# Graph network, three layers of segment maximum: two whole columns of each step fetched row by row by SyncE and ScalarE, their offsets loaded 16 and 32 at a time

## The reference: what is computed

```python
def _sage_conv(x, src, dst, Wl, bl, Wr):
    agg = jax.ops.segment_max(x[src], dst, num_segments=x.shape[0])
    agg = jnp.where(jnp.isfinite(agg), agg, 0.0)
    return agg @ Wl + bl + x @ Wr
...
h = jnp.maximum(_layernorm(x, axis=-1), 0.0)
x = x + _L0_gnn_ref(h, edge_index, ...)     # three _sage_conv, each with a leaky ReLU behind it
```

## Time and profile before

| | |
|---|---|
| median of three runs | 6050.79 us |
| the profiled execution | 6050.56 us, of which the span from first to last instruction is 6048.9 us |
| GpSimd busy | 4524.8 us (75%) |
| VectorE busy | 2893.5 us (48%) |
| ScalarE busy | 225.4 us (4%) |
| TensorE busy (matmul) | 732.5 us (12%) |

### The profile page before, as it was taken

How to read it: one execution, slowest core, us unless ns; L and a number is a source line. 1 busy time by engine, 2 the same in 40 slices (tenths; PEclk the granted TensorE clock), 3 DMA queues, 4 the chain that set the end, 5 groups by cost and what they waited for, 6 DMA issues and landing times.

```text
span 6048.9 us, 53349 instructions
## 1 busy us (share of the span) xinstructions
PE 732.5 (12%) x2214; PEld 411.8 (7%) x2214; DVE 2893.5 (48%) x3638; ACT 225.4 (4%) x664; POOL 4524.8 (75%) x4793
## 2 busy tenths in 40 slices
PE   1111111111100311111111110040010000100003
PEld 0000000000000200000000000030000000000002
DVE  5333333333333555555555555565555555555556
ACT  1000000000000100000000000010000000000001
POOL 6777777777777777777777777767777777777776
PEclk7555555555555655555555555575555555555556
DMA  4333333333333566666666666666666666666665
GB/s 141 108 111 107 108 108 109 110 108 108 108 108 107 171 216 218 218 216 220 216 218 218 216 219 214 215 206 219 217 220 215 218 218 216 220 215 218 215 216 175
DMA packets 461123, 1089.10 MB, mean 180 GB/s; under 512 B 116295, under 2 KB 181740, under 8 KB 461068
## 3 DMA queue, kind: packets, MB, share of 16 engines
q0 software_dynamic: 203520, 519.10, 30.6%
q1 hardware_dynamic: 220508, 544.04, 24.8%
q10 hardware_dynamic: 37040, 25.45, 1.5%
HBM read 555.08 MB, written 533.07 MB: 180 GB/s over the span
## 4 chain that ended last, share of the span: by engine, by line
POOL 49%; issue 17%; DMA 1%; POOLq 1%; DVE 0%; PE 0%; DVEq 0%
POOL ring L448 47%; POOL ring L475 2%; POOLq L444 0%; DMA ring<-running_max_log,end_row 0%; POOLq L441 0%; DMA patch<-running_max_log,patch_row 0%; DMA ring<-features,stage 0%; DMA running_max_log<-patch 0%; POOL patch L465 0%; DVE z_sum L902 0%; DVE agg L894 0%; POOLq L455 0%; POOLq L443 0%; DMA features<-h_out 0%; DVE patch L873 0%
## 5 line engine op out<-in xcount | busy, mean ns | idle before, releaser
L448 POOL DMA_INDIRECT ring<-features,stage x4611 | 4360.0, 946 | 1432.2 <-issue 1383.7
L792 DVE TENSOR_TENSOR ring<-banks,ring 128x1024 f32<-128x1024 f32 (+1 forms) x1173 | 1227.4, 1046 | 2954.0 <-DMA ring<-features,stage 2918.9
L758 DVE TENSOR_TENSOR banks<-ring,banks 128x1024 f32<-128x1024 f32 (+1 forms) x1173 | 1232.1, 1050 | 37.5
L975 PE MATMUL banks<-wr,h_turned 128*128 128x256 f32 (+1 forms) x490 | 220.7, 596 | 3623.4 <-ACT h_turned L1109 3623.4
L975 PEld LDWEIGHTS banks<-wr,h_turned 128*128 128x128 f32 x490 | 127.2, 320 | 3687.4 <-ACT h_turned L1109 3678.6
L991 PE MATMUL banks<-dst_low,own 128*128 128x394 bf16 x200 | 100.4, 502 | 976.0 <-DVE own L734 976.0
L475 POOL DMA_INDIRECT ring<-running_max_log,end_row x147 | 142.9, 972 | 65.6 <-issue 43.9
L1109 ACT ACTIVATE h_turned<-banks 128x256 f32<-128x256 f32 (+1 forms) x147 | 51.8, 353 | 3128.6 <-issue 2664.1
L739 DVE COPY stage<-edges 128x8 int32 (+1 forms) x588 | 119.4, 203 | 88.0 <-DVE banks L758 32.8
L977 PE MATMUL banks<-b,ones 1*128 1x256 f32 (+1 forms) x294 | 157.6, 637 | 0.0
L1048 PE MATMUL banks<-wl,agg 128*128 128x256 f32 (+1 forms) x490 | 110.7, 369 | 1.2 <-DVE agg L894 0.9
(11 more groups left out here) (114 smaller groups left out, 523.4 us busy)
## 6 DMA issues: line engine op xcount, KB each, us to landing
running_max_log<-ring SPq DMA_DIRECT2D x782, 512.0 KB, 3.1
running_max_log<-ring SPq DMA_DIRECT2D x391, 256.0 KB, 2.2
ring<-features ACTq DMA_DIRECT2D x4752, 1.0 KB
ring<-features,stage POOLq DMA_INDIRECT x4611, 3.2
ring<-features SPq DMA_DIRECT2D x3888, 1.0 KB
ring<-features ACTq DMA_DIRECT2D x2376, 0.5 KB
ring<-features SPq DMA_DIRECT2D x1944, 0.5 KB
h_in<-features ACTq DMA_DIRECT2D x98, 128.0 KB, 2.5
```

The costliest lines, as they stand in the source:

```text
L448: pool.indirect_dma_start(ring[0:rows, c * w:(c + 1) * w], None, tables[l], bass.IndirectOffsetOnAxis(ap=stage[0:rows, b, u:u + 1].bitcast ...
L758: dve.tensor_tensor(sum_ps[:, 0:CHAINS * w].rearrange("p (h f) -> p h f", h=CHAINS), group(g - 1).rearrange("p (h f) -> p h f", h=CHAINS), ...
L792: dve.tensor_tensor(group(g), sum_ps[:, 0:CHAINS * w], group(g), ALU.max).then_inc(turn, 1)
L975: pe.matmul(mm_ps[p][:, 0:n], h_turned[p][:, c, :], wr_sb[l][:, c, :], start=(c == 0), stop=False)
```

## The change

Columns 54 and 55 of each full step are fetched row by row as a whole: SyncE fetches the 128 rows of column 55, ScalarE the 128 rows of column 54. GpSimd gathers 54 columns of a full step and no longer the part of column 54. SyncE loads 16 offsets at a time (eight loads in a step, behind the first eight logs), ScalarE 32 at a time (four loads). The offsets of a batch begin at multiples of 16 or 32 of their tensor, and a row of that tensor is 256 words in place of 160. The last step of a layer is as before.

```diff
-SYNC_ROWS, SYNC_AT_ONCE = 72, 8
-ACT_AT_ONCE = 11
-ROWS = 160
+FETCHED_COLS = 2
+SYNC_ROWS = 128
+AT_ONCE, ACT_AT_ONCE = 16, 32
...
+    ROWS = FETCHED_COLS * P
     ROWS_OF = [(0, SYNC_ROWS), (SYNC_ROWS, ROWS - SYNC_ROWS)]
...
-        return width(b, last) - (b == BLOCKS - 1 and not last)
+        return width(b, last) - (FETCHED_COLS if b == BLOCKS - 1 and not last else 0)
...
-            rows = 2 * P - ROWS if c == RING_COLS - 2 and not last else P
             pool.indirect_dma_start(
-                ring[0:rows, c * w:(c + 1) * w], None, tables[l],
+                ring[:, c * w:(c + 1) * w], None, tables[l],
...
-                    first = g * SYNC_AT_ONCE
+                    first = g * AT_ONCE
...
-                            if not last and BLOCK_GROUPS * b * SYNC_AT_ONCE < SYNC_ROWS:
+                            if not last and BLOCK_GROUPS * b * AT_ONCE < SYNC_ROWS:
                                 fetch_rows(i, BLOCK_GROUPS * b)
```

More of the change, by code:

```diff
@@ L87, in gnn_program @@
     assert LAST <= RING_COLS - CHAINS and all(f * (STEPS - 1) < 1 << 16 for f in FETCHED)
-    assert SYNC_ROWS % SYNC_AT_ONCE == 0 and (ROWS - SYNC_ROWS) % ACT_AT_ONCE == 0
-    assert SYNC_ROWS // SYNC_AT_ONCE <= GROUPS - 3
+    assert SYNC_ROWS % AT_ONCE == 0 and (ROWS - SYNC_ROWS) % ACT_AT_ONCE == 0
+    assert SYNC_ROWS // AT_ONCE <= GROUPS - 3
     def by_pool(b, last):
-        return width(b, last) - (b == BLOCKS - 1 and not last)
+        return width(b, last) - (FETCHED_COLS if b == BLOCKS - 1 and not last else 0)
     OPENING = [CHAINS if b == LATE_BLOCK else width(b, True) for b in range(BLOCKS)]
@@ L278, in gnn_program @@
         LAYERS = len(shapes)
-        LOADS = 8
+        LOADS = 6 + FETCHED_COLS
         CONSTS = 16 + 2 * CHAINS
@@ L307, in run_neighbours, with lists_of @@
             return pairs
[L309 to L316, removed]
+        def lists_of(edges_src):
+            return [(row_list[:, k * P:(k + 1) * P],
+                     bass.AP(edges_src.tensor, (CHAINS - 1 - k) * P * RUN + GROUPS - 1, [[GROUPS, STEPS - 1], [RUN, P]]))
+                    for k in range(FETCHED_COLS)]
         def row_places(k, engine, i, at, count, w):
@@ L331, in row_slot @@
         def row_slot(k, r, w):
-            before, p = divmod(ROWS_OF[k][0] + r, P)
-            c = RING_COLS - 1 - before
-            p += before * (2 * P - ROWS)
+            ahead, p = divmod(ROWS_OF[k][0] + r, P)
+            c = RING_COLS - 1 - ahead
             return ring[p:p + 1, c * w:(c + 1) * w].bitcast(U8)
@@ L414, in _ @@
                         pool.dma_start(dest, there).then_inc(sort_done, DMA)
-                pool.wait_ge(list_loaded, 2 * DMA)
+                pool.wait_ge(list_loaded, FETCHED_COLS * DMA)
                 with nc.allow_non_contiguous_dma(reason="one word of each row to fetch"):
-                    for here, there in list_of(sorted_src):
+                    for here, there in lists_of(sorted_src):
                         pool.dma_start(here, there).then_inc(sort_done, DMA)
@@ L446, in gather @@
                             c = b * BLOCK_COLS + u
-                            rows = 2 * P - ROWS if c == RING_COLS - 2 and not last else P
                             pool.indirect_dma_start(
-                                ring[0:rows, c * w:(c + 1) * w], None, tables[l],
+                                ring[:, c * w:(c + 1) * w], None, tables[l],
                                 bass.IndirectOffsetOnAxis(
-                                    ap=stage[0:rows, b, u:u + 1].bitcast(U32), axis=0),
+                                    ap=stage[:, b, u:u + 1].bitcast(U32), axis=0),
                             ).then_inc(late_landed if last and b == LATE_BLOCK and u >= CHAINS else landed[b], DMA)
@@ L689, in _ @@
             dve.memset(restart_turns[:, :, 0], LOWEST).then_inc(prep_done, 1)
-            dve.wait_ge(list_loaded, 2 * DMA)
+            dve.wait_ge(list_loaded, FETCHED_COLS * DMA)
             for w in widths:
@@ L1207, in _ @@
             with nc.allow_non_contiguous_dma(reason="one word of each row to fetch"):
-                for here, there in list_of(src):
+                for here, there in lists_of(src):
                     sp.dma_start(here, there).then_inc(list_loaded, DMA)
@@ L1228, in fetch_rows @@
                             sp.wait_ge(logged[BLOCKS - 1], i * (DMA * STORES_OF[BLOCKS - 1]) + LOGGED[BLOCKS - 1] * l)
-                    places = row_places(0, mybir.EngineType.SP, i, first, SYNC_AT_ONCE, w)
+                    places = row_places(0, mybir.EngineType.SP, i, first, AT_ONCE, w)
                     for r, place in enumerate(places):
@@ L1247, in log_step @@
                                      ).then_inc(logged[b], DMA)
-                        if not last and (BLOCK_GROUPS * b + 1) * SYNC_AT_ONCE < SYNC_ROWS:
+                        if not last and (BLOCK_GROUPS * b + 1) * AT_ONCE < SYNC_ROWS:
                             fetch_rows(i, BLOCK_GROUPS * b + 1)
```

## The result

The changed kernel takes 6475.25 us (median of four runs, 6472.84 to 6482.3) against 6051.17 us for the kernel before (four runs): a ratio of 1.0703, interval 1.0685 to 1.0722. The forecast was 6350 us, in a range of 5945 to 6600. The profiled execution took 6473.37 us. From its page: the span; the groups that answer to the earlier trace rows, with busy time, mean ns, idle time and its releaser; the instruction queue (packets, MB, share); and the logs' KB and us to landing, which answer to the earlier trace rows.

What follows compares the result with a forecast made beforehand. The prediction took GpSimd's gathers to bound the kernel, and the row fetch with its piled logs to bound it afterwards. From 6050.6 us, +332 for layers 2 and 3 and −34 for layer 1 gave 6350 us, range 5945 to 6600.

Steps and rivals of the forecast that it cites:

- the chain: Layers 2 and 3, from row fetch through group 13's log to the next fetch: 76.1 us a round (70.7 to 81.9).
- the burst of six logs: Sign of being right: on SyncE, six logs go out behind its last row, near 65 us of a step.
- SyncE's rows: SyncE's fetch of 128 rows with eight loads of 16 offsets: 63.6 us a step (58.2 to 69.4).
- The piled logs: Logs of groups 8 to 13 queue behind SyncE's rows: 12.5 us from last row to next fetch, layers 2 and 3.
- ScalarE's rows: ScalarE's fetch of 128 rows with four loads of 32: 56 to 72 us, likely 61 to 63.
- GpSimd as the bound before: In the kernel before, GpSimd's 55 gathers of 1.25 us set the step at 68.75 us; the row fetch is hidden.
- The floor of 54 gathers: With one gather fewer, GpSimd alone needs 67.5 us for a full step.
- The sum: Whole kernel against the profiled 6050.6 us: −34 in layer 1, +166 in each of layers 2 and 3, giving 6349.
- the 26 rounds: Layers 2 and 3: 26 rounds lengthened from 68.75 to 76.1 us, 191 us in each layer.
- GpSimd stays the bound: Rival: SyncE's chain in layers 2 and 3 stays under 67.5 us, all 101 us are saved, 5949 us; chance 0.20.
- The two cancel: Rival: loads of 16 take 1.4 us, logs as counted; 6057 us, within 0.2% of no change; chance 0.07.
- A price for each register: Rival: wide loads cost 0.27 us per register, so ScalarE takes 84 us a step; about 7900 us; chance 0.06.

Runs made afterwards that it cites:

- e2: e1 with SyncE's eight batches of rows behind the logs of groups 0, 1, 3, 5, 6, 8, 10 and 11, so nearly none pile up: 6479.32 us.
- e4: The kernel before the change, with only ScalarE's offset loads widened to 32, 32 and 24, aligned, instead of eight of 11: 6054.21 us, ratio 0.9999.
- e1: The changed kernel with 33 do-nothing semaphore increments on SyncE ahead of its first layer, shifting its loops: 6361.42 us, ratio 1.0508.
- e6: e1 with each of SyncE's eight loads of 16 offsets ahead of its log instead of behind it: 6145.06 us, ratio 1.0142.
- e5: The changed kernel with its offsets stored one word further on, so no load begins at a multiple of four words: 7937.73 us in one run.
- e10: e8 with do-nothing semaphore increments on SyncE and ScalarE that shift both engines' loops: 6060.8 us, ratio 1.0011.
- e3: e1 with SyncE loading 32 offsets four times instead of 16 eight times, rows still issued 16 behind each log: 6170.01 us, ratio 1.0189.
- e7: e6 with ScalarE's first load of a step also ahead of its waits: 6086.75 us, ratio 1.0053.
- e11: e10 with SyncE's eight batches behind the logs of groups 0, 1, 2, 4, 5, 7, 8 and 10: 6115.2 us, ratio 1.0103.
- e12: e7 (128 rows on each engine) with SyncE's batches behind the logs of groups 0, 1, 2, 4, 5, 7, 8 and 10: 6177.47 us, ratio 1.0205.
- e9: e8 with 112 rows on SyncE and 144 on ScalarE: 6385.22 us, ratio 1.0549.
- e8: e7 with SyncE fetching 120 of the 256 rows and ScalarE 136: 6163.45 us, ratio 1.0182.

## Why the prediction was right, and what it mis-sized

The mechanism came as forecast. In layer 3, which no refetch disturbs, the chain goes round in 76.0 us against 76.1, and the burst of six logs stands behind SyncE's last row.

- **SyncE's rows.** 47.0 us and eight loads of 2.1 us: 63.6 with the first load. Measured from the first load's start to the last row's end 64.1; the loads 2.15 us at the median, 1.6 in layer 1 (1.8 was taken).
- **The piled logs.** 12.5 us were forecast from the last row to the next fetch; layer 3 has 11.9, which by the forecast's own terms is 1.7 for each of the six logs where 1.8 was taken. The log of group 13 lands 6.8 us behind its issue. e2 shows the mechanism by itself: without the pile that landing is 3.1 us, and the tail 4.1 us shorter.
- **ScalarE's rows.** 61 to 63 us were forecast, 53 to 56 came: the load of 32 was mis-sized, 2.25 us and not 3.3, and the 128 rows without loads take 46 us where their upper bound of 50 was put in. It costs the total nothing, since SyncE ends later.
- **GpSimd as the bound before.** e4 takes 18 us from ScalarE's queue for a ratio of 0.9999. The floor of 54 gathers is seen too: in layer 1 e1's step is 67.4 us.
- **The sum.** e1, the change without refetch, took 6361 us against the 6349 worked out. By layer, from its first row to the next layer's (or to the end): −36, +170 and +172 us in e1's trace, for −34, +166 and +166. In layers 2 and 3 the terms came as well as the sum: the 26 rounds +188 and +192 for +191, the rest −18 and −20 for −25. In layer 1 the sum is right, and equals GpSimd's floor as the prediction noted, but by luck in its terms: the chain was counted at 68.5 us and GpSimd's floor holds the step at 67.4, so the rounds give 35 us in place of 6.5 and the last step 1 in place of 28.
- **What no term had** is the rest, 114 us: SyncE waits for instructions at its branch. It is the whole of the distance from 6361 to 6475. Layer 1 so gained 2 us in place of 34, and layer 2 lost 253 in place of 166. The range held the time, but its upper part stood for dearer loads and not for this.
- **The rivals.** *GpSimd stays the bound* asked for loads of 16 at 1.4 us or less and for logs of a queue at some 1.3 us each. The loads took 2.15 where they stand, and 1.2 once moved ahead of their log (e6), and even then the step stayed at 72.1 us. The logs took 1.7 each, the last landing 6.8 us behind its issue. *The two cancel* asked for loads at 1.4. *A price for each register* came true only without alignment (e5). The prediction says that the unaligned loads before agree with 200 ns for each register; those rows give 0.34 us (3.75/11), and e5 0.26 to 0.28.

The refetch is shown by e1 and e10: fillers that do nothing take it away. Which places of a loop bring it I can't say. By my count of instructions in the traces, the loops of SyncE that stalled (297 to 331 instructions) begin 37 to 78 instructions past a multiple of 128, those that did not (297, 315, 323 or 331) at 5 or at 85 to 118; ScalarE's loops don't follow these bounds (one of 302 instructions stalls at 62 and one does not at 64). SyncE's 221 instructions never stalled. The Trainium skill, "Runtime: NRT & Kernel Launch", section "Instruction fetch mechanics", says that a branch to a target outside the two pages held forces a fetch before execution goes on. The stalls agree in kind; its pages of 256 instructions did not tell, by my count, which loops stall. That the prediction quoted this section for registers and did not apply it to a loop grown from 221 to 331 instructions was an oversight.

Open is by what mechanism group 13 starts 1.5 us behind the last row in some versions and 3 to 5 in others. It is 1.5 where a load stands between the last batch of rows and the log ahead of it (the change, e1, e2). Where SyncE's last batch is issued directly behind its log it is 3.5 in e3, 4.8 in e6, 4.1 in e7, 5.2 in e10, 5.0 in e11 and 2.9 in e12 (means of layers 2 and 3; the last row is ScalarE's in e10 and mostly SyncE's in the others). e1 and e3 have the same logs piled behind the rows and differ in what stands ahead of the last batch, so what stands ahead of that batch has a part.

The stores that move beside the last rows seem to have one too. In e9 ScalarE's rows end last. In its layer 2 the six piled logs were issued 17 us or more ahead of group 13, which starts 1.7 us behind the last row (median); in its layer 3 they were issued 5 to 10 us ahead, and it starts 5.3 us behind. And e12, with two logs behind the rows, has 2.9 where e7, with five, has 4.1. But e11 has two as well, and 5.0. No trace shows when a single row lands, so this stays an argument.

No version beat the kernel before. e10 comes nearest, 0.1% slower with one gather fewer in each step.

## What to carry to other kernels

- Taking work from the engine that is the bound is worth what the engine that takes it over still has to spare **with everything queued behind it**. SyncE had 15 us to spare for 20 us of rows, and the logs behind them added their own: each step saved one gather of 1.25 us and became 7.3 us longer.
- Load many register values in one aligned load, and issue the load before a large store of the same kernel moves, not behind it. Then look for where the gain goes: in e6 the loads among the rows saved 7.1 us and the step fell by 3.9.
- When a loop's body grows, look at the time behind its branch and at the packets of the instruction queue before explaining anything else: here 114 us of 424 were that, and they moved with every edit of e8 and e9.

## What the runs showed of the hardware

- **Loads of offsets** depend on alignment and on what moves beside them: 16 aligned 1.2 us behind rows, 2.15 behind a log, 3.1 behind two; 32 aligned 2.25 us at the median on ScalarE (3.1 to 3.3 in e4, 8.1 beside the piled logs in layer 2 of e7) and 3.05 on SyncE behind a log; 16 and 32 unaligned 4.5 and 8.2 us.
- **Instruction fetch at a loop's branch**: 2.8 to 5.8 us for each turn on SyncE and 3.2 to 5.4 on ScalarE where the loop (297 to 331 instructions) lies in some places, 0.2 in others.
- **Issue of a row** takes 322 ns at the median on SyncE in every version; its mean rises from 329 (e1) to 350 ns (e6) when rows are issued right behind a store.
